# Adaptive feed-forward kernel: group 1 of x by transposes, sums and scaling two blocks at a time, eight weight steps in the tiles

## The reference

```python
q_emb = relu(cond @ W3 + b3)                        # (32, 512)
v     = (64 * x + sum_over_n(x)) * q_emb[:, None]   # x: (32, 64, 512)
h0    = relu(v @ W2 + b2)                           # (32, 64, 512)
w1, w2 = ternary(W_fc), ternary(W_proj)             # groups of 64: sign * mean(abs), or 0
h     = square(relu(h0 @ w1.T))                     # hidden 2048
hn    = h * rsqrt(mean(h * h, -1) + eps)
out   = x + hn @ w2.T
```

## Time and profile before

| what | value |
|---|---|
| time, median of 3 runs | 313.87 us (312.69 to 313.96) |
| the profiled execution | 313.7 us, span 311.9 us |
| PE busy | 306.4 us (98%) |
| DVE busy | 185.3 us (59%) |
| ACT busy | 191.6 us (61%) |
| POOL busy | 102.5 us (33%) |

### The profile page before, as it was taken

How to read it: one execution, slowest core, us unless ns; L and a number is a source line. 1 busy time by engine, 2 the same in 40 slices (tenths; PEclk the granted TensorE clock), 3 DMA queues, 4 the chain that set the end, 5 groups by cost and what they waited for, 6 DMA issues and landing times.

```text
span 311.9 us, 3806 instructions
## 1 busy us (share of the span) xinstructions
PE 306.4 (98%) x1294; PEld 234.6 (75%) x1294; DVE 185.3 (59%) x314; ACT 191.6 (61%) x282; POOL 102.5 (33%) x94
## 2 busy tenths in 40 slices
PE   8999999999999999999999999999999999999995
PEld 7774545446888888888888888888888888888883
DVE  0588899995987968873248225952222484222245
ACT  1696566688999699786445554444555445455540
POOL 1013333235633233353342431154433304443330
PEclk9999999999999999999999999999999999999999
DMA  6997464345754011121003300340000034000003
GB/s 214 353 288 234 120 220 126 96 131 139 210 103 101 1 35 37 34 46 21 2 0 141 130 0 1 117 156 0 0 2 0 0 135 137 0 0 0 2 2 136
DMA packets 31332, 27.03 MB, mean 87 GB/s; under 512 B 18736, under 2 KB 20816, under 8 KB 31312
## 3 DMA queue, kind: packets, MB, share of 16 engines
q1 hardware_dynamic: 29936, 26.22, 28.5%
q10 hardware_dynamic: 1376, 0.56, 0.7%
HBM read 18.39 MB, written 4.19 MB: 72 GB/s over the span
## 4 chain that ended last, share of the span: by engine, by line
PE 98%; DVE 0%; issue 0%; POOL 0%; POOLq 0%; DVEq 0%
PE ps_out L362 37%; PE ps_acc L350 37%; PE ps_acc L334 18%; PE ps_out L307 2%; PE ps_out L323 1%; PE ps_acc L406 1%; PE ps_x L421 1%; PE ps_acc L413 0%; PE ps_x L396 0%; DVE x_sb L569 0%; DVE x_t L499 0%; PE ps_x L402 0%; PE ps_acc L409 0%; POOL ident_f L719 0%; POOL ident_f L717 0%
## 5 line engine op out<-in xcount | busy, mean ns | idle before, releaser
L240 POOL TENSOR_TENSOR wv_sb<-wv_sb 128x512 f32<-128x512 f32 x55 | 71.7, 1304 | 121.3 <-DVE y_lo L514 119.3
L350 PE MATMUL ps_acc<-h_hi,w_t 128*128 128x512 f32 x256 | 100.0, 391 | 0.0
L362 PE MATMUL ps_out<-w_t,y_hi 128*128 128x512 f32 x256 | 100.0, 391 | 0.0
L362 PE MATMUL ps_out<-w_t,y_lo 128*128 128x512 f32 x256 | 99.7, 389 | 0.0
L350 PE MATMUL ps_acc<-h_lo,w_t 128*128 128x512 f32 x256 | 99.6, 389 | 0.0
L512 DVE CAST y_hi<-x_t 128x512 fp32r<-128x512 f32 x64 | 32.1, 502 | 90.0 <-PE ps_out L362 78.2
L662 ACT ACTIVATE x_t<-ps_acc 128x512 f32<-128x512 f32 x64 | 37.9, 592 | 65.1 <-PE ps_acc L350 65.1
L334 PE MATMUL ps_acc<-x_t,wv_sb 128*128 128x512 f32 x128 | 56.3, 593 | 0.3 <-DVE x_t L499 0.3
L350 PEld LDWEIGHTS ps_acc<-h_lo,w_t 128*128 128x128 f32 x256 | 48.1, 188 | 10.2 <-issue 0.2
L350 PEld LDWEIGHTS ps_acc<-h_hi,w_t 128*128 128x128 f32 x256 | 48.0, 188 | 10.2 <-issue 0.2
L362 PEld LDWEIGHTS ps_out<-w_t,y_hi 128*128 128x128 f32 x256 | 48.1, 188 | 9.9
(11 more groups left out here) (61 smaller groups left out, 163.0 us busy)
## 6 DMA issues: line engine op xcount, KB each, us to landing
x_sb<-in_x_dram SPq DMA_DIRECT2D x5, 1024.0 KB, 5.9
raw<-in_L_ffn_W_fc_dram SPq DMA_DIRECT2D x8, 512.0 KB, 6.9
raw<-in_L_ffn_W_proj_dram SPq DMA_DIRECT2D x8, 512.0 KB, 4.3
out_dram<-x_sb SPq DMA_DIRECT2D x16, 256.0 KB, 2.1
x_odd<-in_x_dram SPq DMA_DIRECT2D x2, 1024.0 KB, 7.5
x_sb<-in_x_dram SPq DMA_DIRECT2D x4, 256.0 KB, 4.3
wv_sb<-in_L_cond_W_dram SPq DMA_DIRECT2D x4, 256.0 KB, 8.1
x_t<-in_L_cond_W_dram ACTq DMA_DIRECT2D x1, 512.0 KB, 4.9
```

Source lines behind the costliest of these rows:

```text
L240: engine.tensor_tensor(acc, acc, y_sq[:, v % SQ_RING, :], ALU.add).then_inc(sq_added, 1)
L350: last = pe.matmul(ps_acc[:, (UNITS + v) % ACC_RING, :], w_t[:, j, k * P:(k + 1) * P], part[:, k, g * BANK:(g + 1) * BANK], start=(k == 0 ...
L362: last = pe.matmul(ps_out[:, t, :], part[:, v % RING, t * P:(t + 1) * P], w, start=(opens(v) and part is y_hi), stop=(closes(v) and part i ...
```

## The change

Group 1 is transposed and summed by VectorE as groups 2 and 3 are. VectorE sums and scales two blocks (two PSUM banks, 128x1024) with each instruction, in `sum_and_scale_x`; its sums lie in the columns of `sum_mat`, whose last use is in group 0. TensorE turns all four blocks of group 1 ahead of unit 2, and two blocks each ahead of the first and the third unit in groups 2 and 3. Step 8 moves from unit 15 to tile 1, and steps 9 to 15 one place down; the last two kept pairs go to tiles 19 and 20. SyncE loads x of group 3 one pair earlier.

```diff
-    SUMS_AT = 2
-    STEP_AT_UNIT = {0: 0, 1: 1, 3: 2, 5: 3, 7: 4, 9: 5, 11: 6, 13: 7, 15: 8}
-    STEP_AT_TILE = {1: 9, 3: 10, 5: 11, 10: 12, 12: 13, 14: 14, 16: 15}
-
-    SUMS_OF_UNIT = [[0], [1], [2, 3], []]
-
-    def sums_by_vector(g):
-        return g > 1
-
-    KEEP_AT_TILE = {17: 14, 18: 15}
+    STEP_AT_UNIT = {0: 0, 1: 1, 3: 2, 5: 3, 7: 4, 9: 5, 11: 6, 13: 7}
+    STEP_AT_TILE = {1: 8, 3: 9, 5: 10, 10: 11, 12: 12, 14: 13, 16: 14, 18: 15}
+
+    SUMS_OF_UNIT = [[[], [], [0, 1, 2, 3], []], [[0, 1], [], [2, 3], []], [[0, 1], [], [2, 3], []]]
+
+    KEEP_AT_TILE = {19: 14, 20: 15}
...
-        batch_sum = sb("batch_sum", [P, GB], F32)
...
+        batch_sum = sum_mat[:, 0:2 * GB]
...
                 if i == 0:
                     load_x(2)
-                if i == 2:
+                if i == 1:
                     load_x(3)
...
             for u in range(UNITS):
-                after = u // KD + 1
-                if after < GROUPS and sums_by_vector(after):
-                    for k in SUMS_OF_UNIT[u % KD]:
-                        turn_x(after, k)
-                elif after < GROUPS and u % KD == SUMS_AT:
-                    sum_x(after)
+                g, m = u // KD, u % KD
+                if g + 1 < GROUPS:
+                    for k in SUMS_OF_UNIT[g][m]:
+                        turn_x(g + 1, k)
                 make_h0(u)
...
+            def sum_and_scale_x(g, k):
+
+                at = KD * (g - 1) + k
+                dve.wait_ge(xt_done, KD * g + k + 2)
                 wait(dve, h0_done, KD * (g - 1))
...
+                wait(dve, summed, at)
+                x1 = x1_t[:, g % RING, k:k + 2, :].rearrange("p k (b n) -> p (k b) n", n=N)
+                src = ps_out[:, k:k + 2, :].rearrange("p k (b n) -> p (k b) n", n=N)
+                dve.tensor_reduce(batch_sum[:], src, AX.X, ALU.add).then_inc(summed, 1)
+                dve.wait_ge(summed, at + 1)
+                dve.scalar_tensor_tensor(out=x1, in0=src, scalar=float(N),
+                                         in1=batch_sum[:].rearrange("p (b o) -> p b o", o=1).to_broadcast([P, 2 * GB, N]),
+                                         op0=ALU.mult, op1=ALU.add).then_inc(summed, 1)
+                dve.wait_ge(summed, at + 2)
+                x1 = x1_t[:, g % RING, k:k + 2, :].rearrange("p k (b n) -> p k b n", n=N)
+                dve.tensor_tensor(x1, x1, q_t[:, k:k + 2, g * GB:(g + 1) * GB].rearrange("p k (b o) -> p k b o", o=1)
+                                  .to_broadcast([P, 2, GB, N]), ALU.mult).then_inc(x1_ready, 2)
...
-                if g + 1 < GROUPS and sums_by_vector(g + 1):
-                    for k in SUMS_OF_UNIT[m]:
-                        scale_x(g + 1, k)
-                elif g + 1 < GROUPS and m == SUMS_AT:
-                    for k in range(KD):
-                        scale_x(g + 1, k)
+                if g + 1 < GROUPS:
+                    for k in SUMS_OF_UNIT[g][m][::2]:
+                        sum_and_scale_x(g + 1, k)
```

More of the change, by code:

```diff
@@ L305, in _, with sum_x_block @@
         def _(pe):
-            def sum_x_block(g, t, k):
-                return pe.matmul(ps_out[:, k, t * P:(t + 1) * P], x_of[g % 2][:, t, k * P:(k + 1) * P], sum_mat[:],
+            def sum_x_block(t, k):
+                return pe.matmul(ps_out[:, k, t * P:(t + 1) * P], x_sb[:, t, k * P:(k + 1) * P], sum_mat[:],
                                  start=True, stop=True)
-            def sum_x(g):
-                pe.wait_ge(x_loaded[g % 2], 16 * ((g + 1) // 2))
-                pe.wait_ge(x1_ready, KD * g)
-                for k in range(KD):
-                    for t in range(TT):
-                        last = sum_x_block(g, t, k)
-                    last.then_inc(xt_done, 1)
             def turn_x(g, k):
@@ L425, in _ @@
                 for k in range(KD):
-                    last = sum_x_block(0, t, k)
+                    last = sum_x_block(t, k)
                     if t == TT - 1:
@@ L482, in step @@
                 ternary_pair(i)
-            def scale_x(g, k):
-                dve.wait_ge(xt_done, KD * g + k + 1)
-                wait(dve, h0_done, KD * (g - 1))
[L487 to L501, removed]
@@ new lines, in scale_x @@
+            def scale_x(k):
+                dve.wait_ge(xt_done, k + 1)
+                dve.tensor_tensor(x1_t[:, 0, k, :].rearrange("p (b n) -> p b n", n=N),
+                                  ps_out[:, k, :].rearrange("p (b n) -> p b n", n=N),
+                                  q_t[:, k, 0:GB].rearrange("p (b o) -> p b o", o=1).to_broadcast([P, GB, N]),
+                                  ALU.mult).then_inc(x1_ready, 1)
+            def sum_and_scale_x(g, k):
+                at = KD * (g - 1) + k
+                dve.wait_ge(xt_done, KD * g + k + 2)
+                wait(dve, h0_done, KD * (g - 1))
+                wait(dve, summed, at)
[10 more added lines that the diff above has]
+                                  .to_broadcast([P, 2, GB, N]), ALU.mult).then_inc(x1_ready, 2)
@@ L585, in _ @@
                 dve.wait_ge(q_ready, k + 1)
-                scale_x(0, k)
+                scale_x(k)
             sum_pair(0)
```

## The result

The changed kernel takes 314.60 us in the median (314.38 to 315.96, 20 runs), the kernel before 313.62 (312.69 to 314.78, 20 runs). The ratio is 1.0042, 95% interval 1.0033 to 1.0050. It is slower by 0.98 us by the medians and by 1.3 us by the ratio, inside the half per cent that was called no change. Its profiled execution has a span of 312.9 us against 311.9.

The account below looks back on a forecast made before the run. TensorE bounds the kernel before; VectorE would become the h0 stretch's bound. -1.83 + 0.06 + 1.05 + 0.23 + 0.56 + 0.23 = +0.3 us, forecast 314.1 us from a median of 313.87; range 312.4 to 315.9.

Parts of the forecast that it names:

- What TensorE gains: Group 1 in h0: sixteen transposes at 1.74 us replace fp32 sum matmuls at 3.57 us, 1.83 us less on TensorE.
- The price of a pair: VectorE in h0: summing and scaling two blocks with 128x1024 instructions takes 3.64 us, against 4.10 for two single blocks.
- No gap on VectorE: VectorE works without a gap from 24 to 62 us, its last x1 ready at 62.25 against 60.93 before.
- TensorE's waits: TensorE in h0 waits for x1 1.05 us in unit 4 and 0.56 in unit 12, plus 0.06 for banks.
- The filling behind a wait: TensorE's first 16 instructions after a wait take 0.23 us more, 7.10 in place of 6.87; counted twice.
- The tiles and the loads cost nothing: Moved steps, kept pairs and group 3's load cause no TensorE wait; cover 0.66 us at tile 6, 2.3 at tile 20.
- +0.3 us in all: Sum of TensorE's saving, new waits and filling up to unit 12's end in h0, with no wait behind it.
- Dearer pairs: Rival: two-bank instructions on VectorE cost what two instructions did, 4.10 us a pair, giving 316.9 us; chance 0.14.
- The clock in the new waits: Rival: TensorE's clock falls to half rate in the h0 waits, 3.4 us per unit, 315.8 to 317.5 us; chance 0.04.
- the forecast's 0.34 us for each: VectorE's list ahead of the last x1 in h0: eight roundings at 0.34 us each, 2.72 us together.

Follow-up runs that it names:

- The experiment without the addition: Changed kernel without the instruction for 64 x + sum, so x1 is x times q; 311.91 us, ratio 0.9945 against the kernel before.
- the two single parts: Kernel before with only groups 2 and 3 in pairs of blocks: 313.51 us; kernel before with only the changed kernel's weight-step tables: 313.14 us.
- the experiments on the steps and on the load: Kernel before with the changed weight-step tables alone: 313.14 us; changed kernel with group 3's x load back in its old place: 314.76 us.
- the two order-changed kernels: Changed kernel with each weight step behind its unit's sums: 313.31 us; the same with ScalarE's relu also ahead of the waiting spread: 312.60 us.

## Why the prediction was right, and where its sizes were off

The forecast was 314.1 us, no change; measured 314.6. Its mechanism held: VectorE becomes the bound of the h0 stretch and takes back what TensorE saves. The experiment without the addition shows that the saving is there, and the two single parts show that neither the steps nor the pairs cost anything. That the number came as close as 0.5 us is partly luck: it stands on a median of 313.87 us from three runs, where twenty give 313.62, and measured from there it would have been 313.9, 0.7 us short.

- **What TensorE gains**: 1.83 us forecast; 3.57 to 1.75 in the profile after, and 61.69 to 59.86 us for the stretch where nothing waits for x1.
- **The price of a pair**: 3.64 us forecast, 3.72 measured. The instructions took the 1.22 us of the row they were taken from, but the multiplication starts 0.10 us behind the end of the instruction it waits for (1.33 - 1.23), where the 128x512 block had some 0.04. Six times 0.08 is 0.5 us at the last x1.
- **No gap on VectorE**: as forecast, 24.31 to 71.90 without one.
- **TensorE's waits**: the profile's idle times, 0.85 and 0.76, count from the end of a row, and that end lies 0.16 us behind the place where the next instruction would have started (29.16 + 1.72 = 30.88 against 29.16 + 1.88). Counted as the forecast counts, the waits are 1.01 us in unit 4 (1.05 forecast) and 0.92 in unit 12 (0.56 forecast), with 0.15 us for the banks (0.06) and 0.15 in unit 8 (0). The filling behind a wait took 0.11 us each time, not 0.23. The term that was most undersized is the last wait, by the price of the pairs. The wait in unit 4 would have grown by it too, but in this run TensorE started 0.47 us later and VectorE's first pair only 0.30.
- **The tiles and the loads cost nothing**: right (the experiments on the steps and on the load, and a span longer by 1.0 us with the tiles 1.08 us later).
- **+0.3 us in all**: the step whose size failed. The stretch measured +0.61 us, and the times differ by more still, 1.0 to 1.3. The first hidden tile, forecast at 74.6 to 74.7 against 74.36 in the chain, stands there at 75.44. The term that I did not have is the start. In the kernel before and the two that keep its bound, the first hidden tile comes 61.7 to 61.8 us after the first h0 matmul whether that starts at 11.03, 11.50 or 12.11 us. In the changed kernel and the two that keep its bound it comes at 74.9, 74.8 and 74.5 us for starts at 12.58, 11.58 and 11.46. I had tied VectorE's first pair to 24.01 from a profiled run whose TensorE started late (12.11). A run of before that starts sooner gets the gain; the changed kernel does not, because the first pair waits for VectorE's and ScalarE's list, not for TensorE. The times fit: 18 of the 20 runs of the changed kernel lie between 314.38 and 314.94, those of before between 312.69 and 314.78.
- **What sets that list's start**: in the eight traces that keep this order ahead of it, VectorE's first instruction on group 1 comes 3.89 or 3.90 us after ScalarE begins to read the raw weights of pair 3 (24.31 against 20.41 in the profile after, 24.01 against 20.11 before). That read begins between 20.06 and 20.74 us, each time behind a wait of 0.35 to 0.83 us for the load. So the rows point at the load; no experiment moved it.
- **Dearer pairs**: fell, at 1.23 us an instruction. **The clock in the new waits**: it stayed at its upper level through 0.85 us, so nothing here speaks for the rival of the clock gate. The Trainium skill (TensorE: Matmul & The Clock Gate, "Part 1: The HAM clock gate") says that idle time takes the clock down; it does not say that a wait of a microsecond is enough, and no run here shows the clock fall in the h0 stretch.

## What to carry to other kernels

A share of busy time hides an engine that is full in one stretch: VectorE was at 59% of the span and at 94% from 29.49 to 60.85 us, and this change put 4.8 us more on its list ahead of nearly all of that. Before work moves to a second engine, walk its list up to the piece that the first engine waits for, and look for what may stand behind that piece instead; here the order of the same work was worth 2 us. Put nothing that waits ahead of what frees a buffer of the bound engine: relus behind a waiting spread cost 1.75 us in the h0 stretch, where the late sums cost 2.44 (62.30 - 59.86).

## What the runs showed of the hardware that was not expected

Two roundings in a row on VectorE take 0.76 us (66.78 to 67.54 in the profile after) when the second is issued before GpSimd has begun its subtraction. Ahead of the first pair in the two order-changed kernels they take 2.07 us, and there GpSimd already runs it. VectorE and GpSimd in order of time in the last of them, and the second rounding by itself (the view from 20.55 us on):

```profile
20.07 2.07 DVE L500 CAST h_hi<-h_f 128x512 fp32r<-128x512 f32 x2 [0.96 <-ACT h_f L648]
...
20.64 1.50 DVE L500 CAST h_hi<-h_f 128x512 fp32r<-128x512 f32 x1
...
20.58 1.28 POOL L708 TENSOR_TENSOR h_lo<-h_f,h_hi 128x512 fp32r<-128x512 f32 x1 [18.08 <-DVE h_hi L500]
22.22 1.27 POOL L708 TENSOR_TENSOR h_lo<-h_f,h_hi 128x512 fp32r<-128x512 f32 x1 [0.36 <-DVE h_hi L500]
```

The second rounding takes 1.50 us where 0.42 or 0.43 is usual, and ends at 22.14, 0.28 us behind GpSimd's 20.58 + 1.28 = 21.86. The rest of the 2.07 us is its wait for the relu. The changed kernel has it as well, behind the last x1: a rounding of 1.18 us at 72.77, with GpSimd at work from 72.40 to 73.67. The first y_lo above is another case, 1.67 us for 0.69. The Trainium skill (GPSIMD Engine Reference, "1. Specifications") says that VectorE and GpSimd share their way to SBUF and that VectorE's instructions in a 2-port mode, or with two inputs in SBUF, contend for it. The y_lo, with two inputs in SBUF, agrees. That the rounding is of the first kind is a guess from its time, 0.42 us for 512 elements where a two-input f32 instruction of that size takes 0.69; no trace shows the mode. The f32 sums of 1024 elements from PSUM kept their 1.22 us while GpSimd worked (24.48 to 25.74 in the profile after). So the place of a rounding is worth 1.1 us here, which the forecast's 0.34 us for each did not hold; of the roundings ahead of the changed kernel's last x1, none met it.

The 0.10 us between the end of an instruction and the start of the 128x1024 multiplication by q that waits for it, against 0.03 between the reduction and the instruction behind it, stays unexplained: a pattern with one dimension less did not change it, nor did another instruction in front.
